# Cross-attention with a quantised feed-forward on one core: the opening's transfers, norms and keys in another order

## The reference

```python
def _layernorm(x): return (x - mean(x)) / sqrt(var(x) + 1e-5)

def xattn(query, key, value, mask):
    q, k, v = (split_heads(y @ W + b) for y, W, b in ...)        # B, 16, S, 8
    scores = einsum('bhqd,bhkd->bhqk', q, k) / sqrt(8)
    scores = where(mask == 0, -1e9, scores)
    out = einsum('bhqk,bhkd->bhqd', softmax(scores), v)
    return merge_heads(out) @ Wo + bo

def ffn(x, w1, w2):                                              # rows quantised to 8 bit, weights to -s, 0, s
    return bitlinear(gelu(bitlinear(x, w1)), w2)

x = x + xattn(_layernorm(x), ctx, ctx, mask)
x = x + ffn(_layernorm(x), w1, w2)
```

## Time and profile before

| what | value |
|---|---|
| median of 3 runs | 913.84 us (913.83 to 914.48) |
| the profiled execution, its own time | 913.98 us |
| its span, first to last instruction | 912.3 us |
| PE busy | 841.9 us, 92% of the span |
| DVE busy | 766.7 us, 84% |
| ACT busy | 701.5 us, 77% |
| POOL busy | 303.7 us, 33% |
| mean granted clock of PE | 0.977 of full |

### The profile page before, as it was taken

How to read it: one execution, slowest core, us unless ns; L and a number is a source line. 1 busy time by engine, 2 the same in 40 slices (tenths; PEclk the granted TensorE clock), 3 DMA queues, 4 the chain that set the end, 5 groups by cost and what they waited for, 6 DMA issues and landing times.

```text
span 912.3 us, 33988 instructions
## 1 busy us (share of the span) xinstructions
PE 841.9 (92%) x11724; PEld 634.5 (70%) x11724; DVE 766.7 (84%) x2599; ACT 701.5 (77%) x1272; POOL 303.7 (33%) x360
## 2 busy tenths in 40 slices
PE   1676989999999999999999999999999999999993
PEld 1335767777777777777777777777777777777772
DVE  4887679888898989888898989888898989888954
ACT  1345768978797888979797888979797888979671
POOL 5512352323433333323433333322433333323300
PEclk9888999999999999999999999999999999999996
DMA  5433223343233333343233333343233323340100
GB/s 134 107 78 87 53 65 94 91 101 90 65 92 81 92 82 97 88 106 86 65 90 80 93 80 97 88 107 86 65 91 80 93 80 97 88 108 23 37 2 6
DMA packets 79000, 74.01 MB, mean 81 GB/s; under 512 B 10250, under 2 KB 75258, under 8 KB 78970
## 3 DMA queue, kind: packets, MB, share of 16 engines
q1 hardware_dynamic: 75695, 72.65, 31.0%
q10 hardware_dynamic: 3275, 0.97, 0.5%
HBM read 47.97 MB, written 0.92 MB: 54 GB/s over the span
## 4 chain that ended last, share of the span: by engine, by line
PE 64%; DVE 18%; issue 10%; ACT 3%; ACTq 2%; DMA 1%; DVEq 1%; SPq 1%; POOL 0%; POOLq 0%
PE ps_p L917 10%; PE ps_v L964 10%; PE ps_p L902 10%; PE ps_p L923 6%; PE ps_p L930 6%; PE ps_p L848 6%; PE ps_p L844 6%; DVE spare L1206 4%; PE ps_p L841 4%; DVE mask_bias L1113 1%; DVE row_stat L1025 1%; DVE row_stat L1026 1%; DVE row_stat L1024 1%; PE ps_p L872 1%; PE ps_p L868 1%
## 5 line engine op out<-in xcount | busy, mean ns | idle before, releaser
L1206 DVE CUSTOM_DVE_ANT_0 spare<-ps_p,mask_bias 120x500 bf16<-120x500 f32 x744 | 467.3, 673 | 49.0 <-PE ps_p L902 38.3
L737 ACT ACTIVATE probs<-ps_p 125x448 f32<-125x448 f32 x768 | 352.5, 559 | 57.1 <-PE ps_p L930 53.1
L621 POOL TENSOR_TENSOR k_lo<-k_full,keys 128x500 fp32r<-128x500 f32 x96 | 127.5, 1328 | 255.6 <-ACT keys L727 238.8
L917 PE MATMUL ps_p<-qry_lo,keys 64*125 64x448 f32 x768 | 162.8, 418 | 7.7 <-DVE seg_max L1206 2.6
L902 PE MATMUL ps_p<-keys,qry_hi 64*120 64x500 f32 x768 | 157.5, 430 | 5.6 <-DVE seg_max L1206 5.4
L964 PE MATMUL ps_v<-probs,vals 125*32 125x112 f32 x6144 | 160.7, 260 | 0.3 <-ACT probs L737 0.3
L964 PEld LDWEIGHTS ps_v<-probs,vals 125*32 125x32 f32 x6144 | 145.2, 110 | 22.4 <-issue 22.1
L923 PEld LDWEIGHTS ps_p<-qry_hi,keys 64*125 64x125 f32 x1536 | 146.0, 184 | 8.5
L930 PE MATMUL ps_p<-own_query,mask_bias 57*125 57x448 f32 x768 | 144.8, 370 | 7.5 <-DMA own_query<-shift 7.5
L923 PE MATMUL ps_p<-qry_hi,keys 64*125 64x224 f32 x1536 | 145.6, 266 | 0.0
L917 PEld LDWEIGHTS ps_p<-qry_lo,keys 64*125 64x125 f32 x768 | 72.5, 182 | 64.9 <-DVE seg_max L1206 33.0
(11 more groups left out here) (127 smaller groups left out, 885.1 us busy)
## 6 DMA issues: line engine op xcount, KB each, us to landing
keys<-k_lo SPq DMA_DIRECT2D x384, 62.5 KB, 2.0
ctx_sb<-in_ctx_dram SPq DMA_DIRECT2D x31, 750.0 KB
mask_sb<-in_mask_Bx1xSxS_ik_dram SPq DMA_DIRECT2D x64, 328.1 KB
own_query<-shift SPq DMA_DIRECT2D x64, 1.8 KB
out_dram<-x_rows SPq DMA_DIRECT2D x16, 56.0 KB, 1.6
ctx_sb<-in_ctx_dram ACTq DMA_DIRECT2D x3, 250.0 KB
x_rows<-in_x_dram SPq DMA_DIRECT2D x1, 672.0 KB, 12.7
w_sb<-in_L_ffn_w_dram SPq DMA_DIRECT2D x2, 256.0 KB, 7.2
```

The lines of the kernel that those rows point to most:

```text
L621: pool.tensor_tensor(k_lo[:, (p + n) % 2, :], k_full[:, (p + n) % 2, :], keys[:, p, 0, at].bitcast(F32), ALU.subtract)\
L737: act.activation(probs[:, (c + NG * p) % NP, h], ps_p[0:KC, BANK[how]["S", c, h], 0:HC], ACT.Exp)\
L917: pe.matmul(score_bank(c, h, how), keys[rows, p, 0, at], qry_lo[rows, p, :, :], start=True, stop=False, skip_group_check=True)
L1206: dve.tensor_tensor_reduce(junk, ps_p[0:MROWS, BANK[how][slot], 0:SEG], mask_bias[0:MROWS, p, s * SEG:(s + 1) * SEG].bitcast(F32), 1.0, LO ...
```

## The change

It changes the opening alone; the loop stays as it is.

- ACT issues the keys' weights first, then the three pieces of context 0, and no more. The query weights and biases go to SP's queue, behind the first tiles of x, in 8 DMAs instead of 12. ACT does one small copy that brings its table in early.
- SP places the keys of batch 0 ahead of the context of batch 1, and the keys of batch 1 ahead of the context of batch 2. The shift of batch 0 stands behind that context; w1, w2 and the rows of Wo behind the shift.
- DVE does the norms in a group of 4 tiles and one of 12, the second behind the first `q_flag`. The normalised tiles lie in a part of `probs` that is free until the first exponentials.
- PE's order of T, X, Q, K and M in "open" and "lead" is another, and its wait for the rows of Wo moves to the words W.

```diff
 PE_PASS = passes(
-    "T0 X0 T1 T2 Q0 Q1 K0 F0 K1 K2 X1 Q2 Q3",
-    "M0 M1 T0 M2 T1 X2 M3 T2 Q4 Q5 M4 K0 M5 M6 K1 M7 X3 M8 K2 Q6 Q7 M9 V0 M10 F0 V1 M11 V2 R0",
+    "T0 T1 T2 X0 K0 Q0 Q1 K1 F0 K2",
+    "M0 X1 M1 Q2 Q3 T0 M2 T1 X2 M3 T2 Q4 Q5 M4 K0 X3 M5 K1 Q6 Q7 M6 K2 M7 V0 M8 M9 V1 M10 F0 V2 M11 R0",
...
 DVE_PASS = passes(
-    "norm1 Q0 Q1 some F0 bias0 norm2 bias1 bias2 Q2 Q3",
-    "m0 m1 norm3 m2 m3 m4 m5 Q4 Q5 m6 m7 m8 m9 m10 m11 m12 m13 some m14 m15 Q6 Q7 "
+    "Q0 Q1 some F0 bias0 norm1 bias1 bias2",
+    "m0 m1 Q2 Q3 m2 m3 m4 m5 m6 m7 Q4 Q5 m8 m9 m10 m11 Q6 Q7 m12 m13 some "
...
+            wq_groups = wq.rearrange("k (h g r) -> k g h r", h=2, g=2)
+            bq_groups = bq.rearrange("(h g r) -> h r g", h=2, g=2)
+            for a in range(2):
+                for g in range(2):
+                    sp.dma_start(wq_sb[:, g, :].rearrange("k (h a r) -> k h a r", h=2, a=2)[:, :, a, :],
+                                 wq_groups[:, g]).then_inc(wq_loaded, 16)
...
             sp.dma_start(x_rows[:, 4:NT], x_groups[:, 4:NT]).then_inc(x_loaded[1], 16)
-            sp.wait_ge(ctx_loaded[0], 16)
+            for n in range(NSEG):
+                place_keys(batch(0, 0), n)
             sp.wait_ge(mask_edge[1], 2)
             load(batch(0, 1))
             sp.dma_start(wv_sb[:], wv).then_inc(wv_loaded, 16)
-            sp.dma_start(w1_sb[:], w1.rearrange("(a p) i -> p a i", p=128)).then_inc(ff_loaded, 16)
-            sp.dma_start(w2_sb[:], w2).then_inc(ff_loaded, 16)
-
-            for n in range(NSEG):
-                place_keys(batch(0, 0), n)
             sp.dma_start(wo_sb[:], wo).then_inc(wo_loaded, 16)
...
+            for n in range(NSEG):
+                place_keys(batch(0, 1), n)
             load(batch(0, 2))
+            place_shift(batch(0, 0))
+            sp.dma_start(w1_sb[:], w1.rearrange("(a p) i -> p a i", p=128)).then_inc(ff_loaded, 16)
+            sp.dma_start(w2_sb[:], w2).then_inc(ff_loaded, 16)
             sp.wait_ge(halves_known, 1)
...
-            for n in range(NSEG):
-                place_keys(batch(0, 1), n)
-            place_shift(batch(0, 0))
             step(batch(0, 0))
...
+            act.wait_ge(consts, 1)
+            act.activation(warm[:], ones_f[0:1, 0:1], ACT.Copy)
             act.wait_ge(wk_loaded, 32)
...
-                dve.wait_ge(x_loaded[min(g, 1)], 16)
-                if g > 1:
-                    dve.wait_ge(xn_copied, g - 1)
-                statistics(chain(group_step, 20 * g), x_rows[:, 4 * g:4 * g + 4, :], xn_stat[:], 4)
+                first, tiles = (0, 4) if g == 0 else (4, NT - 4)
+                dve.wait_ge(x_loaded[g], 16)
+                st = xn_stat[:, :, first:first + tiles]
+                statistics(chain(group_step, 20 * g), x_rows[:, first:first + tiles, :], st, tiles)
```

More of the change, by code:

```diff
@@ L142 @@
 ACT_PASS = passes(
-    "T0 X0 T1 T2 sum kf0 kh0 kf1 kh1 kf2 kh2 X1",
-    "T0 T1 X2 T2 sum kf0 kh0 kf1 kh1 X3 kf2 kh2 V0 V1 V2",
+    "T0 T1 T2 X0 kf0 kh0 sum kf1 kh1 kf2 kh2",
+    "X1 T0 T1 X2 T2 sum kf0 kh0 X3 kf1 kh1 kf2 kh2 V0 V1 V2",
     ACT_EVEN, ACT_ODD, "G0", {"e11": "abs"}, {})
 DVE_PASS = passes(
-    "norm1 Q0 Q1 some F0 bias0 norm2 bias1 bias2 Q2 Q3",
-    "m0 m1 norm3 m2 m3 m4 m5 Q4 Q5 m6 m7 m8 m9 m10 m11 m12 m13 some m14 m15 Q6 Q7 "
-    + " ".join(f"m{n}" for n in range(16, 20)) + " F0 m20 m21 m22 m23 neg R0 bias0 bias1 bias2",
+    "Q0 Q1 some F0 bias0 norm1 bias1 bias2",
+    "m0 m1 Q2 Q3 m2 m3 m4 m5 m6 m7 Q4 Q5 m8 m9 m10 m11 Q6 Q7 m12 m13 some "
+    + " ".join(f"m{n}" for n in range(14, 20)) + " F0 m20 m21 m22 m23 neg R0 bias0 bias1 bias2",
     DVE_EVEN, DVE_ODD, "own D0 O0 rows0 rows1 H0 hid0 hid1 hid2 hid3 U0 Y0",
@@ L246, in xattn_ffn @@
         spare = sb("spare", [128, 2 * 4 * (D + PAIR)])
-        xn = spare[0:PAIR, 0:2 * 4 * D].rearrange("p (a r d) -> p a r d", a=2, d=D)
-        xn_stat = sb("xn_stat", [PAIR, 12, 4])
+        xn_stat = sb("xn_stat", [PAIR, 12, NT])
+        warm = sb("warm", [1, 1])
         xnt = spare[:, 2 * 4 * D:].rearrange("p (a n) -> p a n", a=2)
@@ L275, in xattn_ffn @@
             .rearrange("p (b k) -> p b k", b=NBANK)
+        xn = probs[:].rearrange("p n h c -> p (n h c)")[0:PAIR, NBANK * SEG:NBANK * SEG + NT * D]\
+            .rearrange("p (t d) -> p t d", d=D)
         max_junk = spare[:].bitcast(BF16)[0:MROWS, 0:NBANK * SEG].rearrange("p (b k) -> p b k", b=NBANK)
@@ L506, in _ @@
             sp.dma_start(x_rows[:, 0:4], x_groups[:, 0:4]).then_inc(x_loaded[0], 16)
+            wq_groups = wq.rearrange("k (h g r) -> k g h r", h=2, g=2)
[4 more added lines that the diff above has]
+                                 wq_groups[:, g]).then_inc(wq_loaded, 16)
+                for h in range(2):
+                    at = SLOT * h + GR * a
+                    sp.dma_start(bq_sb[at:at + GR, :], bq_groups[h], allow_slow_non_contiguous=True).then_inc(wq_loaded, 16)
             sp.wait_ge(mask_edge[0], 2)
@@ L540, in _ @@
             sp.wait_ge(stored, 16 * NT)
-        N_WQ = 12
+        N_WQ = 8
         N_WO = 3
@@ L664, in _ @@
         def _(act):
+            act.dma_start(wk_sb[:], wk).then_inc(wk_loaded, 16)
+            act.dma_start(bk_sb[:], bk.rearrange("(p a) -> p a", a=1)).then_inc(wk_loaded, 16)
             ctx_0 = ctx_flat[0:SK * D].rearrange("(c k d) -> k c d", k=KC, d=D)
@@ L669, in _ @@
                     .then_inc((ctx_loaded[0], ctx_second, ctx_third)[n], 16)
[L670 to L680, removed]
             def sum_mask(bt):
@@ L805, in fill @@
                     pe.wait_ge(wtern_ready, n + 1)
+                    pe.wait_ge(wo_rows_loaded, 16 * N_WO_ROWS)
                 if kind == "V" and n == 0 and how == "lead":
@@ L987, in _ @@
             step(batch(-1, 1), "lead")
-            pe.wait_ge(wo_rows_loaded, 16 * N_WO_ROWS)
             steps(pe, step)
@@ L1036, in norm_group @@
             def norm_group(g):
-                dve.wait_ge(x_loaded[min(g, 1)], 16)
-                if g > 1:
-                    dve.wait_ge(xn_copied, g - 1)
-                statistics(chain(group_step, 20 * g), x_rows[:, 4 * g:4 * g + 4, :], xn_stat[:], 4)
-                for r in range(4):
-                    ins = dve.tensor_scalar(xn[:, g % 2, r, :], x_rows[:, 4 * g + r, :], xn_stat[:, 6, r:r + 1],
-                                            xn_stat[:, 11, r:r + 1], ALU.subtract, ALU.mult)
-                ins.then_inc(xn_ready, 1)
+                first, tiles = (0, 4) if g == 0 else (4, NT - 4)
+                dve.wait_ge(x_loaded[g], 16)
+                st = xn_stat[:, :, first:first + tiles]
+                statistics(chain(group_step, 20 * g), x_rows[:, first:first + tiles, :], st, tiles)
+                for t in range(tiles):
+                    ins = dve.tensor_scalar(xn[:, first + t, :], x_rows[:, first + t, :], st[:, 6, t:t + 1],
+                                            st[:, 11, t:t + 1], ALU.subtract, ALU.mult)
+                    if t % 4 == 3:
+                        ins.then_inc(xn_ready, 1)
             def quantise_rows(st, part):
```

2 lines of the change are left out of this document (1 added, 1 removed).

## The result

The changed kernel takes **930.12 us** (median of 4 runs, 929.59 to 930.53) against 914.16 for the kernel before in the same comparison (4 runs, 913.83 to 918.41): a ratio of 1.0164, 95% interval 1.014 to 1.0188 (the two medians alone make 1.0175). It is slower. The forecast was 926.2 with a range of 917.5 to 931, so the sign and the path were right and the size was short by 3.9 us. The profiled execution took 930.11 with a span of 928.0 (before: 913.98 and 912.3).

The account below looks back on a forecast made before the run. TensorE sets the pace after the opening, so the median shifts with f0: context 1 late, batch 1's q_flag at 67.1, keys 77.2, context 2 at 87.2, f0 at 91.2, 12.4 us later: 926.2, range 917.5 to 931.

Parts of the forecast that it names:

- the second context as the last to come: Before the first closing score matmul: context 2, issued at 77.2, lands at 87.2, with the shift hidden at 86.6.
- f0: First closing score matmul of batch 0 on TensorE; forecast at 91.2 against 78.78, its shift added to the median.
- the landing: Contexts 1 and 2, from issue on SP's queue to arrival: 10 us each, bounds 8.7 to 11.2.
- T0 of batch 1 to q_flag: PE's opening work on batch 1: 20.9 us against 23.9 before, low end 18 with PE at full clock.
- T0 of batch 2 to f0: PE's transposes of batch 2 ahead of f0: 4.0 us against 3.0 before, at a lower clock after idling.
- The third piece of context 0: Start of the opening, ahead of the first projection: landing left at 18.29, could be there at 9 to 10.
- q_flag to the last placing of keys: POOL and SP placing batch 1's keys: 10.1 us as before, ending at 77.2.
- Norms in 4 and 12: DVE's group of 12 behind the first q_flag: 9.7 us, ending about 36.9, covered by the wait for context 1.
- (a): Ahead of f0: the shift comes last, not context 2; f0 at 86.6, 7.8 later, 921.6; chance 0.12.
- (b): Whole opening: all low ends at once, f0 at 80.8, time 915.8; chance 0.09.
- (c): Opening: not slower, context 0 by 12.2 and contexts landing in 8.2; f0 at 77.6, 912.7; chance 0.07.
- (d): Behind f0: batch 2's keys and masks start late, first pair of steps waits another 4 or more; 930; chance 0.06.

Follow-up runs that it names:

- e1: The changed kernel with the context and masks of batch 2 issued ahead of batch 1's keys again; 918.94 us, ratio to before 1.0036.
- e3: The changed kernel with the shift of batch 0 issued ahead of context 2; 932.61 us, ratio to before 1.0179.
- e7: The changed kernel with the two masks of batch 2 moved behind the shift; 928.84 us, ratio to before 1.0145.
- e8: The changed kernel with contexts 1 and 2 each loaded in two DMAs, of 112 and 13 partitions; 916.65 us, ratio to before 1.0023.
- e4: The kernel before with only contexts 1 and 2 moved behind the keys, as in the change; 932.06 us, ratio 1.0185.
- e9: e6 with contexts 0, 1 and 2 cut into DMAs of 112 and 13 partitions; 894.9 us, ratio to before 0.9783.
- e2: The changed kernel with contexts 1 and 2 both issued ahead of the keys they stood behind; 910.94 us, ratio to before 0.9948.
- e6: e2 with the shift of batch 0 right behind segment 0 of batch 1's keys; 903.4 us, ratio to before 0.987.
- e5: The kernel before with the shift of batch 0 right behind segment 0 of batch 1's keys; 909.71 us, ratio 0.9941.
- e10: e5 with contexts 0, 1 and 2 cut into DMAs of 112 and 13 partitions; 906.3 us, ratio to before 0.9912.

## Why the prediction was right, and short by 4 us

**What bounds the opening, and the second context as the last to come.** Right. f0 sets the time: over the kernels of the table it goes from 74.50 to 97.63, and the median less f0 stays between 834.2 and 837.6. e1 shows that context 2 is what f0 waits for, e3 that the shift is not.

**The term that was mis-sized: the landing.** I took 10 us, with a bound of 11.2. It is 11.75 and 11.90, outside that bound, which makes 3.65 of the 3.92 us that f0 came later than forecast. That so little else is left is luck in part: the issue of context 1 came 1.37 late, T0 of batch 1 to q_flag was 1.64 shorter and T0 of batch 2 to f0 0.54 longer, and these three cancel.

The start of the transfer was not misread: the rate climbs over the first 2.3 us in the earlier trace rows and over 2.4 us in the changed kernel. What I left out stands at its end. In the trace of before the last of the 1500 rows of that same load ends at 87.75, 10.0 us after its issue, but the last raise of its semaphore comes at 88.86, 11.1 us after. My 10 us were the bytes without the raise. In e7 it is 9.5 for the last row and 10.8 for the last raise. In the changed kernel the last raise comes 11.85 us after the issue; where its 0.7 us above before arise is not shown.

The rate of 108 GB/s itself was right. I took it for what the queues share; the five engines stood beside it in the prediction as a page's rule, and I did not put the two together. e8 shows that the rate goes with the number of engines.

**The third piece of context 0.** Left at 18.29; it came at 19.61, 1.3 late, which SP's freedom at 37.52 (forecast 36.2) repeats. e4, e7 and e8 have 19.3 to 20.2 and e9, with the contexts cut, 8.90: it was held up by the shape of 125 partitions, not by its competitors alone. My low bound of 9 to 10 was a real one, for a reason that I had not named.

**T0 of batch 1 to q_flag of batch 1.** 19.26 instead of 20.9, within its bounds. In e8, where T0 does not wait, it takes 16.25, under my low end of 18. Stretches of 4 us, of the changed kernel and then of e8 (busy PE, PEld, DVE, ACT, POOL; granted clock, DMA share, GB/s), show where 3 us of it lie:

```profile
46.00:50.00 4.00, 0.68 (x4) 0.69 (x4) 0.00 (x0) 0.00 (x0) 0.00 (x0) 0.54 0.75 155
50.00:54.00 4.00, 4.00 (x17) 2.54 (x17) 1.51 (x5) 1.72 (x3) 0.00 (x0) 0.50 0.08 22
54.00:58.00 4.00, 4.00 (x10) 1.90 (x10) 2.54 (x7) 2.02 (x3) 0.00 (x0) 0.68 0.00 0
```

```profile
46.00:50.00 4.00, 4.00 (x17) 2.00 (x17) 3.82 (x11) 2.59 (x5) 0.00 (x0) 1.00 0.07 14
50.00:54.00 4.00, 3.57 (x14) 1.36 (x12) 2.40 (x7) 3.75 (x5) 1.79 (x2) 1.00 0.02 4
```

After its wait for context 1 PE works at 0.50, the lower level of 1.2 GHz, until some point between 54 and 58; without the wait it works at 1.00. In both kernels the clock had risen in the stretch from 42 to 44 (means of 0.76 and 0.81); in the changed kernel PE then stands idle for 5.89 us, and the stretch from 46 to 48 shows 0.59. The four transposes of T0 take 1.09 here and 0.62 in e8. Here the late context costs its delay and then the slow stretch behind it.

**q_flag to the last placing of keys.** 10.10 us (78.68 less 68.58), forecast 10.1.

**T0 of batch 2 to f0.** 4.54, forecast 4.0: eight transposes take 1.93 instead of 1.04, at a clock of 0.50 as I had argued, a little more than I allowed. Stretches of 2 us of the changed kernel:

```profile
90.00:92.00 2.00, 1.43 (x7) 1.43 (x8) 0.00 (x0) 0.29 (x1) 0.00 (x0) 0.50 0.67 187
92.00:94.00 2.00, 2.00 (x11) 1.91 (x9) 0.00 (x0) 0.88 (x2) 0.00 (x0) 0.50 0.37 108
```

**Norms in 4 and 12.** The group of 12 took 13.2 us instead of 9.7:

```profile
27.94 2.41 DVE L1012 BATCH_NORM_STATS2 xn_stat<-x_rows 112x6 f32<-112x128 f32 x12
...
36.61 4.54 DVE L1046 TENSOR_SCALAR probs<-x_rows,xn_stat 112x128 f32<-112x128 f32 x12
```

It ends at 41.15. The wait of M2 for DVE is gone, as forecast, and X1 waits for the norms in its place; in the changed kernel the wait for context 1 covers that. With the contexts early the cover is gone: in e2 X1 stands 6.30 us for the norms, until 40.26, and T0 starts only at 45.04. I had said that at most 5 us would show in that case; how much of the 6.30 another grouping would win was not tried.

**The rivals.** (a) falls with e3, (b) and (c) with the landings of 11.8, (d) with the distances behind f0, which are those of before to within 1 us: 930 came from the landings, not from a later stall. The time came out at the price that (d) named, by another mechanism. What (c) said of its place, that the landing of context 1 decides, is half of it: context 1 early is worth 8.0 us (e2 against e1), context 2 early some 11 (e1). In e8, where both land sooner, the change is slower by only 0.23%.

**What stays open.** Why a context takes some 2 us to reach its rate, and why its last raise comes about a microsecond behind its last row, no run shows. The keys ahead of it are not needed for the slow start: in the earlier trace rows nothing moves in the first half microsecond, and the rate climbs just as slowly. A cut in two that leaves each part on few engines, as a check on e8, was not tried.

## What to carry to other kernels

When a load moves behind work that waits for another engine, add its whole landing, from its issue to its reader, to the path, and look for a slow stretch of TensorE behind the wait (3 us here). Take the landing to the reader's start and not to the last byte: the two were 1.1 to 1.3 us apart here. Read the share of DMA engines beside the rate: 100 GB/s at a share of 0.3 is not a full memory path but a shape that uses few engines, and a cut by partitions (112 and 13 for 125) made it 6.3 us instead of 11.9. An opening has several edits that hide each other: the weights, norms and orders here were worth 2 us at most behind late contexts (after against e4), 6 with early ones (e6 against e5) and 11 with short ones (e9 against e10).

## What the runs showed of the hardware

- SP's long issue belongs to the DMA in front, not to the one issued: behind a context of 125 partitions two masks take 6.36 us to issue in the changed kernel, and in e7, where the shift (two DMAs of 1.8 KB) stands there instead, its two issues take 6.83. Behind a context cut into 112 and 13 the same masks take 0.81 (e8). The cut does not free SP everywhere: in the opening of e9, with x and a mask in front as well, the part of 13 partitions takes 6.22 us to issue.
- The same bytes in the same 512-byte rows moved at about 100 GB/s in one DMA of 125 partitions and at up to 353 GB/s in two of 112 and 13. From 72 to 74 us e8 moves no packet of 2 KB or more, so the masks (rows of 6000 bytes) have no part in that rate.
- A DMA raises its semaphore in parts: for 125 partitions once soon after the issue and five times at the end, for 112 sixteen times at the end, for 13 once and then thirteen times. From the last row to the last raise of a context it took 1.1 us in before (87.75 to 88.86) and 1.3 us in e7 (88.27 to 89.57).
